# Self attention of a perceiver block: queries and keys produced transposed, tanh part mixed by itself, scores of two heads in one stationary operand

## The reference

```
Q = heads(Wq, bq); K = heads(Wk, bk); V = heads(Wv, bv)
scores = jnp.einsum('bhid,bhjd->bhij', Q, K) / scale
QJ = jnp.einsum('bhid,hde->bhie', jnp.tanh(Q), J_attn)
delta = jnp.einsum('bhie,bhje->bhij', QJ, jnp.tanh(K))
scores = scores + lambda_attn * delta
scores = jnp.where(causal, -jnp.inf, scores)
probs = jax.nn.softmax(scores, axis=-1)
out = jnp.einsum('bhij,bhjd->bhid', probs, V)
```

## Time and profile before

| | us |
|---|---|
| median of 3 runs | 1328.34 |
| lowest and highest of them | 1325.62 and 1330.13 |
| the profiled execution | 1323.34 |
| its span, from the first to the last instruction | 1320.9 |
| PE busy in the span | 1159.4 |
| DVE busy in the span | 980.3 |
| ACT busy in the span | 661.9 |

### The profile page before, as it was taken

How to read it: one execution, slowest core, us unless ns; L and a number is a source line. 1 busy time by engine, 2 the same in 40 slices (tenths; PEclk the granted TensorE clock), 3 DMA queues, 4 the chain that set the end, 5 groups by cost and what they waited for, 6 DMA issues and landing times.

```text
span 1320.9 us, 49683 instructions
## 1 busy us (share of the span) xinstructions
PE 1159.4 (88%) x20184; PEld 927.4 (70%) x20184; DVE 980.3 (74%) x2496; ACT 661.9 (50%) x1441; POOL 450.4 (34%) x436
## 2 busy tenths in 40 slices
PE   4689999999999999999999999999999875899940
PEld 3577777777777777777777777777777654588830
DVE  6578888888888888888888788878887743465547
ACT  1455555555555555555555555555555532355520
POOL 1333333333333333333333333333333321255530
PEclk8899999999999999999999999999999986799975
DMA  4101111111111111121111111111110004586558
GB/s 162 41 23 46 51 51 50 51 51 51 50 51 50 51 51 35 35 97 37 35 35 35 34 35 35 34 35 35 35 39 15 14 14 135 150 246 169 156 190 269
DMA packets 82559, 91.80 MB, mean 69 GB/s; under 512 B 17248, under 2 KB 72544, under 8 KB 82016
## 3 DMA queue, kind: packets, MB, share of 16 engines
q1 hardware_dynamic: 70816, 65.41, 17.0%
q0 software_dynamic: 6912, 19.01, 4.0%
q10 hardware_dynamic: 4608, 4.20, 0.9%
HBM read 61.19 MB, written 33.78 MB: 72 GB/s over the span
## 4 chain that ended last, share of the span: by engine, by line
PE 67%; DVE 11%; issue 8%; ACT 8%; DMA 3%; POOL 1%; SPq 1%; DVEq 0%; ACTq 0%; POOLq 0%
PE ringB L492 17%; PE ringC L503 11%; PE oA L587 10%; DVE mx L1224 6%; PE banksS L788 5%; PE banksS L570 4%; ACT qT L876 4%; PE ringB L668 3%; PE oA L492 2%; DVE rz L1238 2%; ACT pT L920 2%; PE ringB L622 2%; DMA out<-ksq 2%; PE banksS L639 2%; PE banksS L563 2%
## 5 line engine op out<-in xcount | busy, mean ns | idle before, releaser
L1045 POOL TENSOR_TENSOR kn<-kc,rr 128x512 f32<-128x512 f32 x64 | 66.8, 1065 | 309.8 <-DVE rr L1212 309.8
L503 PE MATMUL ringC<-wx_kv,ct 128*128 128x256 f32 x512 | 158.6, 310 | 8.6 <-DVE ws_down L1366 6.1
L868 ACT ACTIVATE pt<-banksS 128x1024 f32<-128x1024 f32 x128 | 127.6, 1023 | 70.6 <-PE banksS L570 67.0
L1224 DVE TENSOR_REDUCE mx<-banksS 128x8 f32<-128x2048 f32 x64 | 146.4, 2287 | 0.9 <-PE banksS L544 0.9
L503 PE MATMUL ringC<-wx_kv_rest,ct 128*128 128x256 f32 x512 | 145.4, 284 | 0.0
L503 PE MATMUL ringC<-wx_kv,ct_rest 128*128 128x256 f32 x512 | 145.2, 284 | 0.1
L1039 POOL TENSOR_TENSOR sc<-sc,rz 128x1024 f32<-128x1024 f32 x32 | 62.4, 1949 | 197.4 <-DVE rz L1285 197.4
L503 PEld LDWEIGHTS ringC<-wx_kv,ct 128*128 128x128 f32 x512 | 97.9, 191 | 22.4 <-DVE ws_down L1366 6.2
L1082 POOL DMA_INDIRECT expert_rows<-kc,row_to x80 | 76.5, 956 | 69.1 <-DVE kc L1473 62.3
L503 PEld LDWEIGHTS ringC<-wx_kv_rest,ct 128*128 128x128 f32 x512 | 98.3, 192 | 0.1
L503 PEld LDWEIGHTS ringC<-wx_kv,ct_rest 128*128 128x128 f32 x512 | 98.1, 192 | 0.0
(11 more groups left out here) (226 smaller groups left out, 2938.7 us busy)
## 6 DMA issues: line engine op xcount, KB each, us to landing
ct_in<-in_ctxT SPq DMA_DIRECT2D x64, 256.0 KB, 3.0
pt<-rows_by_expert SPq DMA_DIRECT2D x80, 130.0 KB
rows_by_expert<-in_pad_rows SPq DMA_DIRECT2D x16, 260.0 KB
xt<-in_x SPq DMA_DIRECT2D x32, 128.0 KB, 3.3
rows_without_experts<-base SPq DMA_DIRECT2D x32, 128.0 KB
pt<-expert_rows SPq DMA_DIRECT2D x16, 256.0 KB, 3.8
out<-ksq ACTq DMA_DIRECT2D x32, 128.0 KB, 3.8
rows_by_expert<-in_dump_rows SPq DMA_DIRECT2D x1, 2080.0 KB
```

What stands on the lines that cost most here:

```text
L503: mm = pe.matmul(ringC[:, half * DIM:(half + 1) * DIM], left[:, p, k, j // 2, (j % 2) * P:(j % 2 + 1) * P], right[:, k, part * DIM:(part + ...
L868: act.activation(pt[:, g, :, :, :, :].rearrange("p i q c n -> p i (q c n)"), banksS[:, :, g * 256:(g + 1) * 256], ACT.Exp)\
L1045: pool.tensor_tensor(kn[:, 2 * jj:2 * jj + 2, :].rearrange("p j (h d) -> p (j h) d", d=HD), kc[:, 2 * jj:2 * jj + 2, :].rearrange("p j (h ...
L1224: dve.tensor_reduce(mx[:, 2 * r:2 * r + 2, :, 0].rearrange("p q i -> p i q"), banksS[:, :, :].rearrange("p i (q m) -> p i q m", q=2), AX.X ...
```

## The change

The queries and keys are produced with their 256 values on the partitions: in `self_qk` the weights are now the stationary operand, eight blocks of 128x128, and `x1T` moves. So nothing is transposed behind it: `heads_turned`, `heads_in`, and the uses TQ and TK are gone. `self_split` adds a bias for each partition (a column) and writes `qk_linear`; `self_tanh` writes `qk_tanh`, a tensor of its own. `self_mix` mixes the tanh part alone, in two blocks instead of four. Eight heads of 16 values now lie in 128 partitions, so that 32 partitions hold two heads. To keep two heads apart in one product, ACT writes each query twice into `q_parts`, once for the even and once for the odd heads, with the other head's rows multiplied by zero: `queries_apart` from `qk_linear` and `mixed_in` from the mixed tanh part, two instructions each. The scores of the two heads then come from one product with 128 stationary columns (64 queries of the even head, 64 of the odd one) and 64 moving keys; the linear and the tanh part are two such products, summed in PSUM. The scaling of `jmix` has gone into the columns that ACT multiplies by.

The diff's core; what is left out are declarations, the host's layout of the arrays, another way to write `claim`'s search, and the reuse of the freed tensors in the expert stage:

```diff
-                product(bankB("QK"), "QK", lambda k: x1T[:, k, :], wa_qk, 2 * DIM)
-
-            def heads_turned(b, p, u, side):
-                claim(pe, B_USES, B_BANKS, u, b)
-                pe.wait_ge(ev["tanh_ready"].sem, ev["tanh_ready"].of(b))
-                for q4 in range(QG):
-                    mm = pe.transpose(bankB(u)[:, q4 * P:(q4 + 1) * P], qkn[:, side, 4 * q4:4 * q4 + 4, :].rearrange("p h d -> p (h d)"), ident[:, :])
-                mm.then_inc(full[u].sem, 1)
+                for f in range(2 * G):
+                    for k in range(KD):
+                        mm = pe.matmul(bankB("QK")[:, f * P:(f + 1) * P], wa_qk[:, k, f * P:(f + 1) * P], x1T[:, k, :],
+                                       start=(k == 0), stop=(k == 1))
+                mm.then_inc(full["QK"].sem, 1)
...
-                pe.wait_ge(free["TQ"].sem, free["TQ"].of(b))
-                for q4 in range(QG):
-                    mm = pe.matmul(bankB("MIX")[:, q4 * P:(q4 + 1) * P], jmix[:, q4, :], qk4[:, 0, q4, :], start=True, stop=True)
+                pe.wait_ge(ev["tanh_ready"].sem, ev["tanh_ready"].of(b))
+                for g in range(G):
+                    mm = pe.matmul(bankB("MIX")[:, g * P:(g + 1) * P], jmix[:, g, :], qk_tanh[:, g, :], start=True, stop=True)
...
-                for g in range(G):
-                    for bb in range(2):
-                        at = (2 * g + bb) * N
-                        for odd in range(2):
+                for part, keys in enumerate((qk_linear, qk_tanh)):
+                    for g in range(G):
+                        for bb in range(2):
+                            at = (2 * g + bb) * N
                             for i in range(4):
-                                lo, q4 = 32 * i, 2 * g + odd
-                                mm = pe.matmul(banksS[odd * N:(odd + 1) * N, i, at:at + N], qm[lo:lo + 32, q4, bb * N:(bb + 1) * N],
-                                               qk4[lo:lo + 32, 1, q4, bb * N:(bb + 1) * N], start=False, stop=True, skip_group_check=True)
+                                lo = 32 * i
+                                mm = pe.matmul(banksS[:, i, at:at + N], q_parts[lo:lo + 32, part, 2 * g + bb, :],
+                                               keys[lo:lo + 32, G + g, bb * N:(bb + 1) * N], start=False, stop=(part == 1), skip_group_check=True)
...
-            def heads_in(b, p, u, side):
-                act.wait_ge(full[u].sem, full[u].of(b))
-                freed(act, full[("MIX", "SS")[side]], b)
-                act.copy(qk4[:, side, :, :].rearrange("p q n -> p (q n)"), bankB(u)).then_inc(free[u].sem, 1)
+            def queries_apart(b, p):
+                act.wait_ge(free["QK"].sem, free["QK"].of(b))
+                freed(act, full["SS"], b)
+                for odd in range(2):
+                    ins = act.activation(q_parts[:, 0, :, odd * N:(odd + 1) * N], qk_linear[:, 0:G, :].rearrange("p g (b n) -> p (g b) n", n=N),
+                                         ACT.Identity, bias=cols[:, 17:18], scale=cols[:, 15 + odd:16 + odd])
+                ins.then_inc(ev["linear_ready"].sem, 1)
...
-                act.copy(qm[:, :, :].rearrange("p q n -> p (q n)"), bankB("MIX")).then_inc(free["MIX"].sem, 1)
+                for odd in range(2):
+                    ins = act.activation(q_parts[:, 1, :, odd * N:(odd + 1) * N], bankB("MIX")[:, 0:DIM].rearrange("p (q n) -> p q n", n=N),
+                                         ACT.Identity, bias=cols[:, 17:18], scale=cols[:, (6, 18)[odd]:(7, 19)[odd]])
+                ins.then_inc(free["MIX"].sem, 1)
...
-                freed(dve, full["TQ"], b)
-                freed(dve, full["TK"], b)
-                dve.tensor_tensor(qkn[:, :, :, 0:HD].rearrange("p s h d -> p (s h) d"), bankB("QK").rearrange("p (a d) -> p a d", d=HD),
-                                  rows[:, 4:6, :].rearrange("p s (h d) -> p (s h) d", d=HD), ALU.add).then_inc(free["QK"].sem, 1)
+                freed(dve, ev["linear_ready"], b)
+                freed(dve, ev["tanh_ready"], b)
+                freed(dve, full["SS"], b)
+                dve.tensor_tensor(qk_linear[:, :, :], bankB("QK").rearrange("p (a n) -> p a n", n=P),
+                                  cols[:, 11:15].unsqueeze(2).to_broadcast([P, 2 * G, P]), ALU.add).then_inc(free["QK"].sem, 1)
...
-                    dve.tensor_scalar(jmix[:, :, :], jmix[:, :, :], cols[:, 6:7], None, ALU.mult)
```

66 lines of the change are left out of this document (31 added, 35 removed).

## The result

| | before | after |
|---|---|---|
| median, us | 1328.47 | 1358.48 |
| lowest and highest | 1325.62 and 1330.13 | 1350.95 and 1361.22 |
| profiled execution | 1323.34 | 1361.22 |
| its span | 1320.9 | 1359.4 |

The time after is 1.0219 times that of before (95% interval 1.0172 to 1.0266), 30.0 us more. The forecast was 25.8 more and slower. So the kernel is slower beyond doubt; whether by more or less than 2% the interval leaves open. The two profiled executions lie further apart than the medians, 37.9 us: that of before was faster than the four counted here, that of after is the slowest of its four.

A forecast was written before the change was run, and what follows sets the result against it. PE, busy 88% of the span with short waits, was taken as the bound. A step of +0.88 (0.07 - 0.18 + 0.99) gave +27.3 over 31 steps, once -1.5: 1354.1 us, 1.9% slower; 1339 to 1370 held 0.81.

The forecast's parts named there:

- Projection: Self projection on PE: 16 instructions of 128 columns replace four of 512, 1.78 us instead of 1.71, +0.07 a step.
- Transpositions at nothing on the path: Removing PE's head transpositions (1.04 us) gains 0, as PE then idles 1.3 us for DVE's maxima.
- Mixing -0.18: Mixing on PE: four fewer instructions, 0.44 us, of which 0.18 a step counts before DVE's shift is later.
- Scores +0.99: Self scores on PE: loads of 128 stationary columns set the pitch, 1.83 us instead of 0.84; upper bound +1.14.
- What follows the scores hangs on them: PE's work behind the self scores hangs on PE's order or DVE, so all of the +0.99 is on the path.
- ACT at nothing: ACT's longer mixed copy ends before PE needs it, cost 0; without the cover +0.39 a step.
- Once -1.5: Outside the repeated steps: -0.4 for DVE's scaling at the start, -1.1 in the last tile.
- a granted clock below 1.00 in the steps: Sign of a wrong size: PE's granted clock falling in the steps, with 1.6 us of idle instead of 0.6.
- Hidden loads: Rival: self-score loads hide behind moving columns, scores +0.01, step -0.10, 1323.7 us; chance 0.10.
- Full removal of the transpositions and mixing: Rival: PE's removed work counts in full because the maxima don't hold PE back; step -0.42, 1313.8 us; chance 0.04.
- No overlap: Rival: self-score loads and products wait for each other, scores 2.62 us, step +1.67, 1378.6 us; chance 0.05.
- ACT late: Rival: ACT's longer mixed copy delays the exponentials and PE, +0.39 a step on top, 1366.2 us; chance 0.07.

The follow-up runs named there:

- e1: The changed kernel with eight identity transpositions put back on PE ahead of the maxima's transposition; 1353.11 us, 1.0192 of before.
- e8: The kernel before with only its self scores widened to 128 stationary columns, same moving columns and count; 1351.10 us, 1.0176 of before.
- e3: The changed kernel with half the keys left out of the self scores, 32 moving columns instead of 64; 1351.22 us.
- e4: The changed kernel with the odd heads left out of the self scores, 64 stationary columns instead of 128; 1332.34 us.
- e2: The changed kernel with PE's second rough scores ahead of the self projection and DVE's maxima ahead of the split; 1346.94 us, 1.0136 of before.
- e5: e2 with ACT's linear query copies moved behind the routing exponential; 1326.69 us, 1.0002 of before.
- e7: The changed kernel with one DVE instruction put back, the scaling of jmix by 1.0; 1352.79 us, 1.0185 of before.

## Why the prediction was right, and where it was off

**What bounds the kernel.** PE's order with short waits: right. The step of 32.50 was read from one pair of rows; it is the shortest (32.51), and the typical one takes 32.73. The forecast therefore had a step of +0.88 where the single steps compared give 33.47 - 32.50 = +0.97 and the typical ones +0.73.

**Projection.** 1.78 as said, from 1.71.

**Transpositions at nothing on the path.** Right. PE idles 1.15 (forecast about 1.3), e1 put the eight back at no cost to the step, and from the projection to the maxima's transposition it is now 5.02 instead of 4.95, the 0.07 of the projection.

**Mixing -0.18.** Measured 1.50 against 1.67, -0.17, with the shift arriving last as said (0.21 of waiting).

**Scores +0.99.** This is the one term that was mis-sized by more than 0.1, and its mechanism was right: e8, e3 and e4 show from three sides that the stationary columns make it. The size was 1.95 - 0.84 = +1.11, near the upper bound of +1.14. I had taken turns of 0.111 and one end of 0.05; 0.95 and 1.00 for eight turns are 0.119 and 0.125 each, and the upper bound's 1.00 for eight was the nearer row.
The Trainium skill ("TensorE: Matmul & The Clock Gate", LDWEIGHTS) says that a load's time goes by its stationary columns. e3 and e4 agree in kind; the estimate of 1.71 by that rule, with 107 ns for a load whose record shows 186, was 0.24 short of the 1.95 measured.

**What follows the scores hangs on them.** This was right for the chain, but incomplete: the weighted values of before contained 0.23 us of irregular standstill in a step that went when the scores became slower. That term was missing. It outweighs the +0.12 by which the scores were short: 0.07 - 0.17 + 1.11 - 0.23 = +0.78, against +0.73 measured. This sum sets means beside a median, and leaves out the 0.06 more that after loses behind the cross scores, so it closes to 0.1 and not better.

**ACT at nothing.** The cover held, by 0.1 us. In e2 it was lost, and PE waited 0.17 + 0.24 = 0.41. That this is about the +0.39 named for that case is chance: both waits went in e5, which moves the linear copies and leaves the mixed ones.

**Once -1.5.** This can't be read. In the profiled execution of after the granted clock was 0.88 from 58.4 to 72 us, 1.00 in before; from the last tile's first cross scores it was 0.67 over 59.6 us, 0.79 over 59.1 in before. Up to the fourth tile after lost 5.7 us, and behind those last cross scores 4.0.

**The sum.** 31 x 0.73 = 22.6. e7, without the stretched instructions, is 1.85% or 24.5 us above before; 22.6 - 1.5 = 21.1 leaves over 3 us of this unassigned. After is 30.0 above. The two steps with a stretched instruction are 4.0 and 4.8 longer than the typical one in the profiled execution, which the forecast had not foreseen. A part of the nearness of 25.8 is luck: steps forecast 0.15 too long each against the typical one, 4.7 us in all, stand against these and against what is unassigned. The forecast named a granted clock below 1.00 in the steps as a sign of a wrong size; between 181 and 1057 us it fell once, from 570.1 to 573.6, behind the first stretched instruction. The 1.15 us of waiting ahead of the maxima's transposition did not make it fall.

**The rivals.** Hidden loads: refuted by the 1.95 and by e3. Full removal of the transpositions and mixing: refuted by the 1.15 of idle and by e1. Another order (e5) brought the step to 32.64, 0.09 below that of before, not to the 0.42 of this rival. No overlap: the stretch would be 2.62, and it is 1.95. ACT late: not in after, but in e2.

## What to carry to other kernels

Before work is taken from the busiest engine, look at what that engine waits for next: here 1.04 us of transpositions vanished into a wait for another engine's reduction, and only a change of the order on three engines (e5) turned it into time. The self scores, with few moving columns, were paid by their stationary columns, so that the zeros put there to join two heads were not free. And read a step's length as a median over many steps, not from one: the difference here was 0.23 us in 32.7, a quarter of what was to be forecast.

## What the chip showed that was not expected

PE stands still for reasons that no waiting row names: after 128 scores at 12 ns and 59 weighted instructions at 16 ns it did so for 1.65 us ("issue"), and with 64 scores it still lost 0.23 a step on average. 163 of 165 such standstills came at the same place of every 256 records of PE and PEld. So the number of PE's instructions had a price here beyond their durations.

A DVE instruction of 0.36 us took 2.08 at the same two numbers of DVE's stream in all eight kernels that had 2495 DVE instructions, and in none of the six that had one more. In after, PE's clock dropped to its lower level behind the 1.61 us of idle that this made; in e1 and e5 the same idle time left it at 1.00.

The 64 instructions with 64 stationary columns took 0.84 us where they wrote the two halves of the output partitions in turn, and 1.09 where they wrote one half.
